# A perceiver block on one core: every step of a hand-placed schedule set anew, with the banks of the stages and shifts for the last two tiles

## What is computed

```python
x = x + xattn(layernorm(x), ctx_1024)   # 16 heads of 32, keys = values = context, softmax over 257, then W_out
x = x + attn(layernorm(x))              # low-rank q/k/v (256), rotary part, 16 heads, softmax over 32, then Wo
x = x + ffn(layernorm(x))               # 8 experts, the best one of each row: gelu(x W1 + b1) W2 + b2
```

## Time and profile before

| | |
|---|---|
| median of 3 runs | 841.59 us (838.85 to 842.76) |
| profiled execution, its own time | 840.57 us |
| its span, first to last instruction | 838.4 us |
| mean granted TensorE clock | 0.963 |
| busy: PE, PE weight load, DVE, ACT, POOL | 736.7, 554.2, 586.4, 430.2, 334.3 us |
| set-up and first tiles, to ATT of the second tile | 0 to 113 us |
| ATT of the second tile to ATT of the fifteenth | 113 to 568.4 us |
| rest of the attention and the choice of experts | 568.4 to about 653 us |
| experts | about 653 to 838.4 us |

### The profile page before, as it was taken

The page is one execution under the profiler, slowest core; times in us unless marked ns, Lnnn a source line. Parts: engine busy times, 40 slices in busy tenths (PEclk is TensorE's granted clock), DMA queues, the critical chain, the costliest instruction groups (busy, mean ns, idle before and its releaser), DMA issues. The chain is left out here.

```text
span 838.4 us, 26300 instructions
## 1 busy us (share of the span) xinstructions
PE 736.7 (88%) x10502; PEld 554.2 (66%) x10502; DVE 586.4 (70%) x1184; ACT 430.2 (51%) x1085; POOL 334.3 (40%) x687
## 2 busy tenths in 40 slices
...
GB/s 279 329 149 60 115 138 130 146 143 145 139 152 161 125 148 141 151 149 143 141 141 152 144 146 144 140 152 104 2 226 51 216 381 332 186 154 143 142 116 4
DMA packets 114376, 129.06 MB, mean 154 GB/s; under 512 B 14478, under 2 KB 81294, under 8 KB 114256
## 3 DMA queue, kind: packets, MB, share of 16 engines
...
## 5 line engine op out<-in xcount | busy, mean ns | idle before, releaser
L867 ACT ACTIVATE prob<-scores,negmax 128x257 f32<-128x257 f32 x256 | 118.0, 476 | 41.8 <-DVE negmax L1082 41.1
L531 PE MATMUL stage_banks<-qkv_hi,operand_hi 128*128 128x398 f32 x256 | 97.1, 379 | 4.1 <-DVE operand_lo L1086 3.3
L1072 DVE STREAM_TRANSPOSE k_t<-keys 128x512 f32<-128x512 f32 x128 | 88.9, 696 | 15.3 <-DMA keys<-in_ctx 15.3
L1082 DVE TENSOR_REDUCE negmax<-scores 128x2 f32<-128x514 f32 x128 | 82.1, 683 | 23.2 <-PE scores L582 23.2
L592 PE MATMUL scores<-consts,prob 128*128 128x128 f32 x512 | 85.3, 291 | 13.0 <-ACT prob L867 13.0
L606 PEld LDWEIGHTS att_bank<-prob_t,context 128*32 128x32 f32 x4096 | 46.0, 114 | 73.5 <-ACT prob_t L857 45.0
L606 PE MATMUL att_bank<-prob_t,context 128*32 128x32 f32 x4096 | 60.3, 201 | 36.3 <-ACT prob_t L857 36.3
L1337 POOL COPY plast<-prob 128x2 f32<-128x2 f32 x128 | 24.0, 188 | 161.9 <-ACT prob L867 160.6
L532 PE MATMUL stage_banks<-qkv_lo,operand_hi 128*128 128x398 f32 x256 | 88.2, 345 | 0.0
L533 PE MATMUL stage_banks<-qkv_hi,operand_lo 128*128 128x398 f32 x256 | 87.9, 343 | 0.0
L1634 PE MATMUL stage_banks<-w_all,hidden 128*128 x184 | 82.9, 593 | 0.6 <-ACT hidden L1687 0.6
(11 more groups left out here) (260 smaller groups left out, 1672.3 us busy)
## 6 DMA issues: line engine op xcount, KB each, us to landing
keys<-in_ctx SPq DMA_DIRECT2D x256, 128.0 KB, 4.4
...
```

The lines of the kernel that those rows point to most:

```text
L531: pe.matmul(to, op_hi[op][:, c, :], w_hi[name][:, c, columns], start=(c == 0), stop=False)
L867: act.activation(prob[pair][:, gg, :], scores[:, g, 0:J], ACT.Exp, bias=negmax[b % 2][:, g:g + 1], accum_out=sums[t % 2][:, g, bl:bl + 1]) ...
L1072: dve.transpose(dst, src).then_inc(keys_turned, 1)
L1082: dve.tensor_reduce(negmax[b % 2][:, 2 * pair:2 * pair + 2], scores[:, 2 * pair:2 * pair + 2, 0:J], AX.X, ALU.max, negate=True).then_inc(m ...
```

## The change

All the numbers of the table are new, and so is the bank of two stages. Nothing is added to or taken from the work: each engine issues the same instructions in another order, and the waits follow from the order. `LATER` now has an entry for every stage, each with its own shift for the last two tiles; before, it had five, and RANKED used RANK's shift and ROOT3 used X2's. The core of the diff (of the tables a few lines; the call sites repeat one pattern):

```diff
-X_BIAS, XOUT, X1, ROOT1, SCALE1 = -14, (8, 9, 13, 15), 14, 13, 18
+X_BIAS, XOUT, X1, ROOT1, SCALE1 = -18, (10, 11, 12, 15), 15, 18, 19
...
-LATER = {'OUT': (11, -11), 'X2': (2, -3), 'SCALE3': (20, 12), 'CHOOSE': (11, 14), 'RANK': (26, -7)}
+LATER = {"X2": (-1, -11), "SCALE3": (20, -1), "XOUT": (0, 1), "TURN1": (0, 0), "QKV": (0, -1), "TURN_Q": (0, -1), "TURN_K": (-1, -3),
...
-BANK_OF = {'queries': 1, 'xout': 0, 'norm': 1, 'qkv0': 1, 'qkv2': 0, 'av': 0, 'qkv1': 2, 'q': 2, 'k': 0, 'rank': 0, 'qkv3': 1, 'self': 0}
+BANK_OF = {'queries': 1, 'xout': 0, 'norm': 2, 'qkv0': 1, 'qkv2': 0, 'av': 0, 'qkv1': 2, 'q': 2, 'k': 0, 'rank': 1, 'qkv3': 1, 'self': 0}
...
-MAX_AT = (1, 1)
-KEYS_AT = (4, 8)
-KEYS_LOAD_AT = 8
+MAX_AT = (1, 2)
+KEYS_AT = (6, 8)
+KEYS_LOAD_AT = 6
 TURN_P_AT = (6, 8)
-ATTEND_AT = (8, 12)
-KEEP_AT = (7, 9)
+ATTEND_AT = (10, 11)
+KEEP_AT = (8, 8)
...
-UNIT_AT = (1, 4, 6, 9, 10, 11, 13, 15, 16, 17, 18, 19, 20, 21, 26, 27, 28, 29, 31, 32, 33, 38, 40, 43, 44, 45, 46, 47, 48, 49, 51)
+UNIT_AT = (2, 6, 6, 9, 11, 12, 16, 16, 18, 19, 19, 21, 21, 22, 25, 27, 29, 30, 30, 32, 32, 37, 38, 43, 43, 43, 44, 44, 48, 49, 52)
...
-TABLES_AT = 17
+TABLES_AT = 31
...
-BIAS_LOAD_AT = 8
+BIAS_LOAD_AT = 3
...
-            t = tile_at(step, TURN1)
+            t = tile_at(step, TURN1, LATER["TURN1"])
...
-            t = tile_at(step, RANKED, LATER["RANK"])
+            t = tile_at(step, RANKED, LATER["RANKED"])
```

More of the change, by code:

```diff
@@ L38 @@
 TILE = BT * STEPS
-INVERT, SPREAD_INV, SPREAD_LAST, WEIGH_LAST = -6, -6, -6, -1
-ATT, ATT_INV, ATT_HI, ATT_LO = 1, 1, 2, 8
-X_BIAS, XOUT, X1, ROOT1, SCALE1 = -14, (8, 9, 13, 15), 14, 13, 18
[L42 to L53, removed]
-LATER = {'OUT': (11, -11), 'X2': (2, -3), 'SCALE3': (20, 12), 'CHOOSE': (11, 14), 'RANK': (26, -7)}
-BANK_OF = {'queries': 1, 'xout': 0, 'norm': 1, 'qkv0': 1, 'qkv2': 0, 'av': 0, 'qkv1': 2, 'q': 2, 'k': 0, 'rank': 0, 'qkv3': 1, 'self': 0}
+INVERT, SPREAD_INV, SPREAD_LAST, WEIGH_LAST = -6, 0, -6, 1
@@ new lines @@
+ATT, ATT_INV, ATT_HI, ATT_LO = 1, 3, 3, 5
+X_BIAS, XOUT, X1, ROOT1, SCALE1 = -18, (10, 11, 12, 15), 15, 18, 19
+TURN1, NORM_HI, NORM_LO = 21, 22, 20
+QKV = (23, 24, 25, 27, 28, 29, 30, 31, 33, 34, 35, 36, 37, 38, 39, 42)
+QKV_MOVE, ROTATE, OUT_BIAS = (28, 36, 37, 43), 37, 32
+TURN_Q, Q_MOVE, TURN_K, K_PLACE, K_PLACE_DVE = 37, 35, 39, 44, 19
+SELF, SOFT, SOFT_EXP, SOFT_SUM, SOFT_SCALE, SOFT_TURN, SOFT_PLACE = 45, 48, 47, 51, 52, 54, (51, 52, 53, 59)
+AV, SELF_HI, SELF_LO, OUT, X2, ROOT3 = 64, 68, 70, (88, 90, 91, 96), 99, 99
@@ new lines @@
+SCALE3, CHOOSE, RANK, RANKED = 104, 106, 119, 119
+GATE_KEEP = 48
+QUERIES, QUERIES_MOVE = -55, -56
+MEASURE_X, ROOT_X, SCALE_X = 25, 35, 32
+LAST_STEP = TILE * T + 146
+LATER = {"X2": (-1, -11), "SCALE3": (20, -1), "XOUT": (0, 1), "TURN1": (0, 0), "QKV": (0, -1), "TURN_Q": (0, -1), "TURN_K": (-1, -3),
+         "SELF": (1, -2), "AV": (0, -3), "OUT": (8, -17), "RANK": (27, -15), "ATT_HI": (0, 1), "SCALE1": (0, -1), "NORM_HI": (-1, -4),
+         "Q_MOVE": (1, -5), "K_PLACE": (-2, -3), "SOFT_EXP": (0, -4), "SOFT_PLACE": (-3, -4), "SELF_HI": (1, 1), "INVERT": (4, 4),
+         "SPREAD_INV": (0, 0), "SPREAD_LAST": (0, 6), "ATT": (0, 0), "X1": (0, 0), "NORM_LO": (0, 0), "QKV_MOVE": (0, -1),
+         "K_PLACE_DVE": (0, 0), "SOFT": (-1, -3), "SOFT_SUM": (-2, -4), "SOFT_TURN": (-3, -3), "SELF_LO": (1, -3), "CHOOSE": (12, 10),
+         "RANKED": (30, 6), "WEIGH_LAST": (0, -4), "ATT_INV": (2, 1), "ATT_LO": (2, -1), "ROOT1": (0, 0), "ROTATE": (-3, -1),
+         "OUT_BIAS": (0, -2), "SOFT_SCALE": (-1, -4), "ROOT3": (3, -14), "GATE_KEEP": (5, -1)}
@@ L403, in program @@
                "q": TURN_Q, "k": TURN_K, "self": SELF, "av": AV, "out0": OUT[0], "out1": OUT[0], "rank": RANK}
-    later_of = {"out0": LATER["OUT"], "out1": LATER["OUT"], "rank": LATER["RANK"]}
+    later_of = {"xout": LATER["XOUT"], "norm": LATER["TURN1"], "qkv0": LATER["QKV"], "qkv1": LATER["QKV"], "qkv2": LATER["QKV"], "qkv3": LATER["QKV"],
+                "q": LATER["TURN_Q"], "k": LATER["TURN_K"], "self": LATER["SELF"], "av": LATER["AV"], "out0": LATER["OUT"], "out1": LATER["OUT"],
+                "rank": LATER["RANK"]}
     def stage_step(stage, t):
@@ L678, in stages @@
                 turn_queries(t)
-            t, c = part_at(step, XOUT)
+            t, c = part_at(step, XOUT, LATER["XOUT"])
             if t >= 0:
@@ L694, in stages @@
                 turn(norm_w, bank, norm_turned)
-            t, part = part_at(step, QKV)
+            t, part = part_at(step, QKV, LATER["QKV"])
             if t >= 0:
@@ L711, in stages @@
                 turn(qk[:, 0, :], bank, q_turned)
-            t = tile_at(step, TURN_K)
+            t = tile_at(step, TURN_K, LATER["TURN_K"])
             if t >= 0:
```

88 lines of the change are left out of this document (44 added, 44 removed).

## The result

The changed kernel takes 809.55 us (median of 4 runs, 805.4 to 814.45) against 840.22 for the kernel before (4 runs, 834.84 to 842.76). The ratio is 0.964, with a 95% interval of 0.9596 to 0.9685. The profiled execution took 810.45 us, its span is 808.6 us. The forecast was 807.

The account below looks back on a forecast made before the run. DVE's queue paces the tile's first half, PE the second unless keys are late. Tiles 28.6, set-up 2 and last tile 3 make 33.6 us off the profiled 840.57, giving 807 us; range 796 to 830.

Parts of the forecast that it names:

- The tile: Middle tiles: each gains 2.0 to 2.7 us, 2.2 taken, times 13 periods: 28.6 us.
- The keys' term of 1.4 us: Second half: statistics and SELF_LO move on DVE ahead of late keys, into its wait: 1.4 us less behind the keys.
- OUT0's 0.9: Second half: OUT0's 0.90 us on PE moves into the first half, filling idle time of b0 and b1.
- the order of `attend`: First half: `attend` of p0 moves behind p1's turning and AV, so TURN1 comes 1.1 us earlier.
- The clock: PE's granted clock in b1: about as much idle time, in smaller pieces; a dip priced at half a microsecond.
- The rival "slower": Smaller idle pieces in b1 bring PE's clock down in every tile, into QKV: net 1.2 us lost each, 851 us; chance 0.07.
- The rival "half": b3's keys land 1.5 us later behind an earlier context load; gain 0.7 to 1.2 us a tile, 823 us; chance 0.25.
- The rival "no change": DVE's queue grows, exponentials each 0.7 us later, 1.4 at X1, plus a dip; tiles gain nothing, about 840 us; chance 0.04.
- The set-up: Set-up units moved apart: 2 us gained, with bounds of 7 gained and 5 lost.
- PE waits for weights then, which covers them; uncovered they cost up to 5 us: Set-up: ACT's ten bias issues, 5.7 us, ahead of p0's first copy, are covered by PE's wait for weights.
- The last tile: RANK's bank wait goes, TURN_K moves ahead of QKV13 to QKV15, shorter queue ahead of last ATT: 3 us, bounds 1 and 4.

Follow-up runs that it names:

- e6_keys: Changed kernel with MEASURE_X 27, KEYS_AT (4, 8), MAX_AT (1, 1), so DVE's statistics and low half of self lie behind b3's keys again: 834.4 us.
- e5_out: Changed kernel with OUT0 back at step 86, ahead of b0's scores and behind QKV15: 826.21 us.
- e3_attend: Changed kernel with ATTEND_AT back at (8, 12), attend of p0 ahead of the turning of p1 and AV: 832.53 us.
- e11_before_load4: Kernel before with only KEYS_LOAD_AT at 4 instead of 8, so keys are issued earlier: 835.77 us.
- e9_both: Changed kernel with ATTEND_AT back at (8, 12) and MEASURE_X 27, KEYS_AT (4, 8), MAX_AT (1, 1): 845.58 us.
- e4_banks: Changed kernel with the banks as before, norm in bank 1 and rank in bank 0: 809.54 us.
- e8_load4: Changed kernel with KEYS_LOAD_AT 4 instead of 6, keys issued ahead of x's load and norm_scratch's store: 792.62 us.
- e10_combo: Changed kernel with BIAS_LOAD_AT 8 and KEYS_LOAD_AT 4: 788.52 us.
- e12_two: Kernel before with two numbers changed, ATTEND_AT (10, 11) and KEYS_LOAD_AT 4: 809.0 us.
- e1_bias: Changed kernel with only BIAS_LOAD_AT back at 8 instead of 3: 805.88 us.
- e2_setup: Changed kernel with the set-up's whole table (units, cuts, sums, tables, biases, zeros) as before: 811.38 us.
- e7_turnk: Changed kernel with the last tile's TURN_K shift at 3 instead of -3, behind QKV15 again: 809.33 us, one run.

## Why the prediction was right, point by point

**The tile.** 2.2 us were taken from 2.0 to 2.7, and 2.43 came: 31.5 us and not 28.6. In the tile that was worked through, nearly every place came out: TURN1 at S + 15.1 (15.2 forecast) and released by SCALE1; QKV0 at 17.2 (17.3); RANK at 23.2 with a wait of 0.53 (23.4 and 0.8); QUERIES at 25.5 (25.3); the next S at 32.54 (32.5). DVE waits for keys in 12 of 13 tiles, 1.2 us each (nearly every tile, 1 us).

**The keys' term of 1.4 us** is shown by e6_keys, OUT0's 0.9 by e5_out. That the order of `attend` is worth 1.1 us was too little: e3_attend puts 2.1 us on the way to QKV0, since ACT's fourth placing has moved ahead of the copy and the wait in b0, which the sum left out, counts too. Forward the term came out: QKV0 was at S + 18.37 in an undisturbed tile and is at 17.16, with OUT0's 0.9 us taken in.

**The clock** is the step that was mis-sized, twice. "I price a dip at half a microsecond": e11_before_load4 shows 1.3 to 2.5 us where keys don't hide it, and the one that is left in the changed kernel costs 1.5 (from RANK to the next S 10.83 us and not 9.34, in a tile of 34.95). And the forecast had the dips stay, where seven of eight went. In seven of the twelve tiles from the third to the fourteenth QKV0 was at S + 19.6 to 20.6, not at the 18.4 of the tile that I worked through; and their second half took 15.3 us, not 16.9. The sum came out since both kinds of tile took 35 us: one lost 1.3 us or more to the clock, the other some 1.5 to the keys. It was luck that the tile I chose stood for both. A reader who checks one tile should check one of each kind.

**The rival "slower", by the clock,** had the sign wrong: pieces of idle time of 0.2 to 0.5 us brought the clock down in no tile, and waits of 0.98 and 1.44 us, whose ends lie 2.1 us apart, did so in 7 of 12. The one fall of the changed kernel came behind its longest wait at RANK, 1.36 us. That the idle time in long pieces is the cause is a reading and not shown. It fits e3_attend and e9_both (longer waits at `attend`, five and six falls), e6_keys (waits of some 2 us at RANK with three falls behind them; two more lie in the second tile) and e4_banks, e8_load4 and e10_combo (longest waits of 0.9 to 1.1 us, none). Against it stand e5_out, with waits of up to 1.5 us at RANK and none, e12_two, where of three waits of 1.34 to 1.48 us only one has a fall behind it, and e3_attend itself, where 2.2 us stand in each of 12 tiles and the clock fell in four. It is not shown why the seventh tile of the kernel before, with the same waits as the ninth, keeps its clock.

**The rival "half", by later keys,** didn't come. From SP's issue to the end of DVE's wait it was 7.50 us before (335.09 to 342.59) and is 7.25 (323.46 to 330.71). The rule of the Trainium skill on which it leaned ("DMA: Bandwidth & Descriptors", section "Issuing engines are not separate DMA queues") is not refuted by that: in these two windows the share of the DMA engines was 0.82 and 0.88, 207 and 223 GB/s, so they were hardly busier than before.

**The rival "no change"** asked whether DVE's queue grows. It didn't: X1 came at S + 11.0, where it was at S + 11.3.

**The set-up** is where the forecast failed: 2 us gained, bounds of 7 gained and 5 lost, and 4.0 were lost. One step was "PE waits for weights then, which covers them; uncovered they cost up to 5 us". The ten issues were not covered, and they cost 5.8 us at the first ATT and 7.2 at the second by e1_bias, 3.9 and 5.2 by e10_combo against e8_load4, because behind PE's wait the clock was down in the big products too. The other step is a term put at nothing: the new loops make the old set-up 4.2 us later (e2_setup). Against these stand 7.5 us that the other moves of the table gained in the new loops: 4.2 + 7.2 - 7.5 = 3.9 us.

**The last tile**: 3 forecast, 2.3 measured. By that stretch alone the gain can't be told from chance: it took 265.5 to 269.3 us in e1_bias, e2_setup, e4_banks, e8_load4 and e10_combo, whose edits aim elsewhere. At its place it is seen: SELF came 2.0 us nearer to TURN1 (13.26 us and not 15.27), of which e7_turnk gives 1.3 to TURN_K; 0.4 came ahead of TURN1.
